# Row totals of the attention weights: every second group of four steps summed into one tile by GpSimd

## The chip, the cores and the metric

One core of one Trainium2 chip runs the whole program. The metric is the device time of one execution in microseconds (us); the kernel before is shown by three timed runs and by one profiled execution. The engines are TensorE (PE, its weight loads PEld), VectorE (DVE), ScalarE (ACT), GpSimd (POOL) and SyncE (SP), which only issues transfers here.

## The reference, cut to what matters

The program is one transformer block: a modulated layer norm, causal attention with 32 heads of 32 channels over 2048 rows, a ten-row adapter prefix, a projection, and then a mixture of 8 experts of which each row takes two. Only the attention matters here:

```
scores = einsum('bhqd,bhkd->bhqk', q, k) / sqrt(hd)
scores = where(causal, scores, -inf)
attn   = softmax(scores, axis=-1)
y      = einsum('bhqk,bhkd->bhqd', attn, v)
```

The softmax is computed as exp(score - row maximum), and y is divided at the end by the total of these weights over all keys of a row. The change is in how that total is formed.

## The kernel before

The attention function works on 4 heads at a time (HG = 4) and on two such head groups in one pass of its outer loop, which runs 4 times. A pass has 8 units (`UNITS`): two head groups times four chunks of 512 query rows. A unit with chunk number qc has 4 * (qc + 1) steps, one for each block of 128 keys, so a pass has 80 steps (`STEPS`): 4, 8, 12 and 16, twice. In each unit the last four steps lie on the diagonal: they work on 512, 384, 256 and 128 query columns (`first_column`). There are 320 steps in all.

A step does this, in the order of its queues:
- PE computes the scores of 4 heads (`score`, L1089, and on the diagonal a small mask matmul, L1093) into three PSUM banks. After each it does one matmul of the look-ahead (`look`, `see`, L1066): it computes the scores of a later unit again, only for their row maximum, into three other PSUM banks (`seen`). DVE takes the maximum of each (`largest`, L1233 and L1239) and frees the bank.
- ACT writes exp of the scores into `prob`, a ring of four steps (`RING = 4`, L1201). Step s overwrites what step s - 4 left, so ACT must wait until PE and POOL have read that.
- PE multiplies the weights of the step two before with v (`multiply`, L1107), four heads at once in four strips of 32 columns of the array.
- For the totals, POOL adds the `prob` of an even step and of the odd step after it into a tile `two` (`add_two`, L1331), in two instructions of two heads each (1024 elements a partition, or 512 on the narrow end of the diagonal). Ahead of a pair on the diagonal it clears the columns that the second step lacks (L1328). PE then adds `two` up over the keys by a matmul with a matrix of ones into `total` (`add_up`, L1120), four steps after the pair's last one, in odd steps only. `two` has two buffers: POOL may start pair p only when PE has read pair p - 2.

Once in a unit: ACT copies y and the total out of PSUM; transfers turn the total into a tile in which DVE inverts it and spread it again; DVE multiplies y by the inverse and adds the adapter's part (`divide`, L1277 and L1280, eight steps after the unit's end); POOL splits the result into two parts (`split`, L1337 and L1339) and SP stores them.

Every queue is written out by hand and runs in order. POOL's order in a step is: `finish` (the second half of the last pair in even steps, then a split if one is due), and then the first half of the new pair in odd steps.

## Time and profile before

| what | value |
|---|---|
| median of 3 timed runs | 2748.73 us (2748.05 to 2749.51) |
| profiled execution, its own time | 2739.68 us |
| its span | 2737.9 us |
| PE busy over the span | 91% |
| DVE, ACT, POOL busy over the span | 59%, 39%, 48% |
| mean granted PE clock | 0.949 |

The span runs from the first to the last instruction of the profiled execution, the own time is the device time of the same execution. Attention's steps run from about 882 us to 1980 us of the span. Busy shares are means over stages that have different limits.

### The profile page before, as it was taken

How to read it: one execution, taken by the hardware profiler on the slowest of the kernel's cores; microseconds unless marked ns; L12 is line 12 of the kernel's file. 1: busy time of each engine (PE TensorE's matmuls, PEld its weight loads, DVE VectorE, ACT ScalarE, POOL GpSimd, SP SyncE). 2: the span in 40 equal slices, each digit the busy share in tenths (PEclk: the TensorE clock that was granted, in tenths of full speed). 3: DMA queues.
4: the chain of work that ended last, by engine and by line, in shares of the span. 5: the costliest groups of instructions: out<-in, count | busy, mean ns of one | idle time of the engine just before them, and what ended most of it. 6: DMA issues, size and time to landing. Idle time of an engine off the chain costs nothing. (4 is left out here: it accounts for less than half of the span.)

```text
span 2737.9 us, 40036 instructions
## 1 busy us (share of the span) xinstructions
PE 2484.4 (91%) x13407; PEld 1621.3 (59%) x13407; DVE 1628.2 (59%) x3253; ACT 1055.2 (39%) x1885; POOL 1321.3 (48%) x827
## 2 busy tenths in 40 slices
PE   6789999998758999999999999999879976999996
PEld 4667677777534444444444444444358765888885
DVE  5544555110458777777777777778226654676666
ACT  3421011111331555555555555556501112444443
POOL 4352342000432767676767676667724452333333
PEclk9899999999885999999999999999989977999998
DMA  7356655312743515151515151522176745878875
GB/s 264 108 160 194 180 167 168 93 39 58 259 134 82 132 40 129 44 131 42 130 42 129 43 128 45 120 48 78 48 227 215 184 101 199 306 276 284 295 283 199
DMA packets 231902, 397.20 MB, mean 145 GB/s; under 512 B 44540, under 2 KB 95292, under 8 KB 231620
## 3 DMA queue, kind: packets, MB, share of 16 engines
q1 hardware_dynamic: 204340, 319.62, 40.1%
q0 software_dynamic: 17152, 50.38, 5.3%
q10 hardware_dynamic: 10256, 25.21, 2.8%
q8 instruction: 88, 1.44, 0.2%
q14 instruction: 66, 0.54, 0.1%
HBM read 299.22 MB, written 103.76 MB: 147 GB/s over the span
## 5 line engine op out<-in xcount | busy, mean ns | idle before, releaser
L1201 ACT ACTIVATE t_prob<-t_scores_psum 128x512 f32<-128x512 f32 (+3 forms) x1280 | 610.0, 538 | 435.7 <-PE t_scores_psum L1093 241.9
L1331 POOL TENSOR_TENSOR t_two<-t_prob 128x1024 f32<-128x1024 f32 (+1 forms) x321 | 691.1, 2175 | 165.6 <-ACT t_prob L1201 111.6
L1233 DVE TENSOR_REDUCE t_part<-t_seen_psum 128x1 f32<-128x512 f32 x768 | 479.0, 681 | 141.3 <-PE t_seen_psum L1066 137.2
L1066 PE MATMUL t_seen_psum<-t_k_stack,t_q_stack 97*128 97x512 f32 (+3 forms) x1283 | 522.0, 419 | 40.3 <-DVE t_q_stack L1221 22.5
L1089 PE MATMUL t_scores_psum<-t_q_stack,t_k_stack 98*128 98x512 f32 (+3 forms) x1280 | 502.8, 404 | 9.1 <-ACT t_prob L1201 7.8
L1089 PEld LDWEIGHTS t_scores_psum<-t_q_stack,t_k_stack 98*128 98x128 f32 x1280 | 241.9, 190 | 306.8 <-ACT t_prob L1201 168.7
L1066 PEld LDWEIGHTS t_seen_psum<-t_k_stack,t_q_stack 97*128 97x128 f32 x1283 | 256.7, 201 | 91.8 <-DVE t_part L1233 37.8
L1239 DVE CUSTOM_DVE_ANT_0 t_seen_psum<-t_seen_psum,t_causal 128x128 f32<-128x128 f32 (+3 forms) x515 | 250.4, 504 | 100.7 <-PE t_seen_psum L1066 89.5
L1107 PE MATMUL t_y_acc_psum<-t_prob,t_v 128*32 128x512 f32 (+3 forms) x2576 | 301.5, 540 | 0.0
L1602 PE MATMUL z_acc_psum<-z_e_hi,z_x_hi 128*128 128x512 f32 x576 | 228.1, 396 | 0.0
L1604 PE MATMUL z_acc_psum<-z_e_hi,z_x_lo 128*128 128x512 f32 x576 | 224.9, 390 | 0.0
L1603 PE MATMUL z_acc_psum<-z_e_lo,z_x_hi 128*128 128x512 f32 x576 | 224.6, 390 | 0.0
L602 PE MATMUL f_acc_psum<-hT_hi,f_w_hi 128*128 128x512 f32 x512 | 207.2, 405 | 2.6 <-POOL f_w_lo L472 2.2
L603 PE MATMUL f_acc_psum<-hT_lo,f_w_hi 128*128 128x512 f32 x512 | 202.0, 395 | 0.0
L604 PE MATMUL f_acc_psum<-hT_hi,f_w_lo 128*128 128x512 f32 x512 | 201.7, 394 | 0.0
L482 POOL TENSOR_TENSOR f_y<-f_y,f_y_hi 128x512 fp32r<-128x512 f32 x64 | 83.8, 1310 | 217.4 <-ACT f_y_hi L264 217.1
L264 ACT ACTIVATE f_y_hi<-f_y 128x512 fp32r<-128x512 f32 x64 | 40.4, 631 | 330.5 <-DVEq L411 330.4
L1120 PE MATMUL t_total_psum<-t_two,t_ones 128*32 128x512 f32 (+1 forms) x1296 | 154.9, 550 | 1.9 <-POOL t_two L1331 1.9
L1828 DVE SCALAR_TENSOR_TENSOR z_x_in<-z_acc_psum,z_ids_a,z_gb 128x1024 f32<-128x1024 f32 x36 | 46.0, 1279 | 140.5 <-DMA z_ids_a<-scratch_table 140.5
L1672 ACT ACTIVATE z_x_hi<-z_turned_psum 128x1024 fp32r<-128x1024 f32 x38 | 38.7, 1018 | 224.5 <-PE z_turned_psum L1588 224.5
L1551 PE MATMUL z_acc_psum<-p_hi,z_y_hi 128*128 128x512 f32 x256 | 102.3, 400 | 23.6 <-DMA z_y_lo<-scratch_y_lo 23.6
L1604 PEld LDWEIGHTS z_acc_psum<-z_e_hi,z_x_lo 128*128 128x128 f32 x576 | 108.4, 188 | 23.0
(234 smaller groups left out, 3894.7 us busy)
## 6 DMA issues: line engine op xcount, KB each, us to landing
z_raw<-in_expert_w SPq DMA_DIRECT2D x80, 512.0 KB, 6.7
z_spare<-in_expert_w SPq DMA_DIRECT2D x72, 512.0 KB, 7.3
f_w_raw<-in_wmod SPq DMA_DIRECT2D x8, 2048.0 KB, 9.9
t_q_stack<-scratch_q_hi SPq DMA_DIRECT2D x64, 256.0 KB, 5.0
t_k_stack<-scratch_k_hi SPq DMA_DIRECT2D x64, 256.0 KB, 5.3
f_w_raw<-in_w_attn SPq DMA_DIRECT2D x24, 512.0 KB, 6.9
t_inverse<-scratch_inverse SPq DMA_DIRECT2D x132, 64.0 KB, 2.0
t_y<-scratch_a_y SPq DMA_DIRECT2D x33, 256.0 KB, 4.6
```

The lines of the kernel that those rows point to most:

```text
L602: nc.tensor.matmul(acc[:, n % 2], lhs[0], rhs[0], start=(k == 0), stop=False)
L603: nc.tensor.matmul(acc[:, n % 2], lhs[0], rhs[1], start=False, stop=False)
L1066: nc.tensor.matmul(seen[:, n % BANKS, 0:width], q_stack[par][0:SEEN, h, t0:t0 + P], k_stack[par][0:SEEN, h, c * CH:c * CH + width], start= ...
L1089: last = nc.tensor.matmul(scores[:, score_bank(step, h), c0:CH], k_stack[par][0:TOPS, h, kt * P:(kt + 1) * P], q_stack[par][0:TOPS, h, qc ...
L1107: last = nc.tensor.matmul(y_acc[h * D:(h + 1) * D, c0:CH], v[par][:, kt, h * D:(h + 1) * D], prob[:, step % RING, h, c0:CH], start=(kt == ...
L1201: nc.scalar.activation(prob[:, step % RING, h, c0:CH], scores[:, score_bank(step, h), c0:CH], ACT.Exp, scale=1.0 / math.sqrt(D)).then_inc( ...
L1233: nc.vector.tensor_reduce(dst, seen[:, n % BANKS], AX.X, ALU.max).then_inc(seen_free, 1)
L1239: nc.vector.tensor_tensor_reduce(out=at, in0=at, in1=causal[:, CH - width:CH], scale=1.0, scalar=MASKED, op0=ALU.add, op1=ALU.max, accum_o ...
L1331: nc.gpsimd.tensor_tensor(two[:, pair % 2, heads, c0:CH], a, b, ALU.add).then_inc(two_ready, 1)
L1602: nc.tensor.matmul(acc[:, s, col], x_hi[:, s, k], e_hi[:, k, col], start=(k == 0), stop=False)
L1603: nc.tensor.matmul(acc[:, s, col], x_hi[:, s, k], e_lo[:, k, col], start=False, stop=False)
L1604: last = nc.tensor.matmul(acc[:, s, col], x_lo[:, s, k], e_hi[:, k, col], start=False, stop=(k == KC - 1))
```

## The change

The 80 steps of a pass are now taken in 20 groups of four (`QUADS`). An odd-numbered group is done as before: two sums of two steps each. An even-numbered group (`long`) becomes one sum of four steps: POOL adds the first two steps as before, then adds the third and the fourth step into the same tile (`add_more`, two instructions for each step, each over the columns that the step has), and PE adds the tile up once, four steps after the group's last step. A pass so has 30 sums where it had 40, and 100 POOL additions where it had 80. In each pass the even groups are 0, 2, 10 and 12, which are a unit's diagonal, and 4, 6, 8, 14, 16 and 18, which have 512 columns in all steps. ACT's waits follow: step s waits for what has been added of step s - 4.

```diff
-                if step % 2 == 1:
-                    add_up(i, (step - TOTAL_LAG - 1) // 2)
+                quad, at = divmod(step - TOTAL_LAG, 4)
+                if at == 3:
+                    add_up(i, quad, 0 if long(quad) else 1)
+                elif at == 1 and not long(quad):
+                    add_up(i, quad, 0)
...
-                    if step % 2 == 0:
-                        act.wait_ge(two_ready, (i * PAIRS + step // 2) * 2 + 2)
+                    quad, at = divmod(step - RING, 4)
+                    if at != 1 and (at != 3 or long(quad)):
+                        act.wait_ge(two_ready, i * HALVES + halves_of(quad) + {0: 2, 2: 4, 3: 6}[at] + 4)
...
+            def add_more(i, quad, x, half):
+
+                n = i * SUMS + sum_of(quad)
+                c0 = first_column(4 * quad + x)
+                heads = slice(half * HALF, (half + 1) * HALF)
+                pool.wait_ge(exp_done, (i * STEPS + 4 * quad + x) * HG + (half + 1) * HALF + BANKS)
+                pool.wait_ge(two_ready, i * HALVES + halves_of(quad) + 2 * (x - 2) + half + 1 + 4)
+                at = two[:, n % 2, heads, c0:CH]
+                nc.gpsimd.tensor_tensor(at, at, prob[:, (4 * quad + x) % RING, heads, c0:CH], ALU.add).then_inc(two_ready, 1)
...
             def finish(i, step):
-                if step % 2 == 0:
-                    add_two(i, step // 2 - 1, 1)
+                quad, at = divmod(step - 2, 4)
+                if at == 0:
+                    add_two(i, quad, 0, 1)
+                elif at == 1 and long(quad):
+                    add_more(i, quad, 2, 0)
+                    add_more(i, quad, 2, 1)
+                elif at == 2 and i * STEPS + step > 0:
+                    if long(quad):
+                        add_more(i, quad, 3, 0)
+                        add_more(i, quad, 3, 1)
+                    else:
+                        add_two(i, quad, 1, 1)
                 for wi in ended(i, step, SPLIT_LAG):
                     split(i, wi)
...
-                    if step % 2 == 1:
-                        add_two(i, step // 2, 0)
+                    if step % 4 == 1:
+                        add_two(i, step // 4, 0, 0)
+                    if step % 4 == 3 and not long(step // 4):
+                        add_two(i, step // 4, 1, 0)
```

POOL's queue, from the pairs of steps 12 to 17 of the first pass (the row with x6) to the pair of steps 22 and 23; group 4 is steps 16 to 19, and steps 20 to 23 are the diagonal of the same unit. Before:

```order
L1331 TENSOR_TENSOR t_two<-t_prob 128x1024 x6
L1337 CAST t_y_own<-t_y 128x512
L1339 TENSOR_TENSOR t_y<-t_y,t_y_own 128x512
L1331 TENSOR_TENSOR t_two<-t_prob 128x1024 x2
L1328 MEMSET t_prob 128x4x128
L1331 TENSOR_TENSOR t_two<-t_prob 128x1024 x2
L1328 MEMSET t_prob 128x4x128
L1331 TENSOR_TENSOR t_two<-t_prob 128x2x256 x2
```

The same piece of POOL's queue in the changed kernel, where L1344 is `add_two`, L1354 `add_more`, L1340 the clearing and L1362 and L1364 the split:

```order
L1344 TENSOR_TENSOR t_two<-t_prob 128x1024 x6
L1354 TENSOR_TENSOR t_two<-t_two,t_prob 128x1024 x2
L1362 CAST t_y_own<-t_y 128x512
L1364 TENSOR_TENSOR t_y<-t_y,t_y_own 128x512
L1354 TENSOR_TENSOR t_two<-t_two,t_prob 128x1024 x2
L1340 MEMSET t_prob 128x4x128
L1344 TENSOR_TENSOR t_two<-t_prob 128x1024 x2
L1340 MEMSET t_prob 128x4x128
L1344 TENSOR_TENSOR t_two<-t_prob 128x2x256 x2
```

Two instructions of 1024 elements in `two` (steps 18 and 19 into one buffer) have become four, and the split now stands between the additions of step 18 and those of step 19.

PE's queue at the end of step 21 of the same pass, before:

```order
L1073 MATMUL t_seen_psum<-t_ident,t_top 16x128
L1066 MATMUL t_seen_psum<-t_k_stack,t_q_stack 128x512
L1107 MATMUL t_y_acc_psum<-t_prob,t_v 32x512 x4
L1120 MATMUL t_total_psum<-t_two,t_ones 32x512 x4
L1089 MATMUL t_scores_psum<-t_q_stack,t_k_stack 128x256
```

And in the changed kernel, where the same functions stand five lines further down:

```order
L1078 MATMUL t_seen_psum<-t_ident,t_top 16x128
L1071 MATMUL t_seen_psum<-t_k_stack,t_q_stack 128x512
L1112 MATMUL t_y_acc_psum<-t_prob,t_v 32x512 x4
L1094 MATMUL t_scores_psum<-t_q_stack,t_k_stack 128x256
```

The four matmuls of the sum of steps 16 and 17 are gone from step 21; the one sum of group 4 stands at the end of step 23, where the sum of steps 18 and 19 stood.

## Rows read from the trace of the kernel before

**Rows 1.** The page, part 1: busy us (share), instructions.

```profile
PE 2484.4 (91%) x13407; PEld 1621.3 (59%) x13407; DVE 1628.2 (59%) x3253; ACT 1055.2 (39%) x1885; POOL 1321.3 (48%) x827
```

**Rows 2.** Windows of attention: width, then busy of the engines (instructions), PE clock.

```profile
core 0: us, PE busy (x) PEld busy (x) DVE busy (x) ACT busy (x) POOL busy (x), PEclk, DMA share, GB/s
1000.00:1200.00 200.00, 197.35 (x1286) 95.47 (x1283) 148.90 (x341) 116.17 (x247) 140.89 (x85) 1.00 0.35 84
...
1900.00:1950.00 50.00, 44.20 (x280) 18.10 (x283) 23.58 (x53) 34.30 (x69) 40.58 (x20) 1.00 0.27 76
```

**Rows 3.** Timeline of PE, steps 17 to 19 of the second pass.

```profile
1210.78 1.06 PE L1107 MATMUL t_y_acc_psum<-t_prob,t_v 128*32 128x512 f32 x8
1211.66 1.04 PE L1120 MATMUL t_total_psum<-t_two,t_ones 128*32 128x512 f32 x8
...
1214.55 1.06 PE L1107 MATMUL t_y_acc_psum<-t_prob,t_v 128*32 128x512 f32 x8
...
1217.46 1.06 PE L1107 MATMUL t_y_acc_psum<-t_prob,t_v 128*32 128x512 f32 x8
```

**Rows 4.** Timeline of PE, steps 12 to 15: after a diagonal.

```profile
1194.98 0.64 PE L1107 MATMUL t_y_acc_psum<-t_prob,t_v 128*32 128x256 f32 x8
1197.63 0.43 PE L1107 MATMUL t_y_acc_psum<-t_prob,t_v 128*32 128x128 f32 x8
...
1200.93 1.06 PE L1107 MATMUL t_y_acc_psum<-t_prob,t_v 128*32 128x512 f32 x8
...
1204.89 0.61 PE L1120 MATMUL t_total_psum<-t_two,t_ones 128*32 128x256 f32 x8
```

**Rows 5.** Groups of POOL by form, 880 to 1990 us: busy, mean ns.

```profile
L1331 POOL TENSOR_TENSOR t_two<-t_prob 128x1024 f32<-128x1024 f32 x256 | 608.6, 2399 | 162.9 <-ACT t_prob L1201 111.6 <-PE t_total_psum L1120 48.7
L1331 POOL TENSOR_TENSOR t_two<-t_prob 128x512 f32<-128x512 f32 x64 | 81.3, 1290 | 2.6
```

**Rows 6.** Timeline of POOL, second pass: steps 17 to 22, then 25 and 29.

```profile
1212.88 4.74 POOL L1331 TENSOR_TENSOR t_two<-t_prob 128x1024 f32<-128x1024 f32 x2 [1.40 <-PE t_total_psum L1120]
1219.06 0.61 POOL L1337 CAST t_y_own<-t_y 128x512 fp32r<-128x512 f32 x1 [1.44 <-DVE t_y L1280]
...
1221.00 4.71 POOL L1331 TENSOR_TENSOR t_two<-t_prob 128x1024 f32<-128x1024 f32 x2
1226.96 0.53 POOL L1328 MEMSET t_prob<- 128x512 f32 x1 [1.25 <-PE t_total_psum L1120]
1227.57 4.73 POOL L1331 TENSOR_TENSOR t_two<-t_prob 128x1024 f32<-128x1024 f32 x2
...
1239.55 4.75 POOL L1331 TENSOR_TENSOR t_two<-t_prob 128x1024 f32<-128x1024 f32 x2 [3.41 <-ACT t_prob L1201]
...
1253.09 4.74 POOL L1331 TENSOR_TENSOR t_two<-t_prob 128x1024 f32<-128x1024 f32 x2 [1.40 <-PE t_total_psum L1120]
```

**Rows 7.** Timeline of ACT: the exps of steps 21 and 24.

```profile
1223.20 1.76 ACT L1201 ACTIVATE t_prob<-t_scores_psum 128x384 f32<-128x384 f32 x4 [1.12 <-PE t_scores_psum L1093]
...
1233.38 2.07 ACT L1201 ACTIVATE t_prob<-t_scores_psum 128x512 f32<-128x512 f32 x4 [2.17 <-PE t_scores_psum L1089]
```

**Rows 8.** Timeline of DVE: the divides at steps 19 and 31.

```profile
1217.05 1.12 DVE L1277 TENSOR_TENSOR t_y_own<-t_y_own,t_inverse 128x512 f32<-128x512 f32 x1
1218.20 0.69 DVE L1280 TENSOR_TENSOR t_y<-t_y,t_y_own 128x512 f32<-128x512 f32 x1
...
1257.26 1.12 DVE L1277 TENSOR_TENSOR t_y_own<-t_y_own,t_inverse 128x512 f32<-128x512 f32 x1
```

**Rows 9.** Timeline of POOL and DVE, 1944 to 1951 us.

```profile
1944.88 5.15 POOL L1331 TENSOR_TENSOR t_two<-t_prob 128x1024 f32<-128x1024 f32 x2 [0.96 <-PE t_total_psum L1120]
1945.56 2.25 DVE L1277 TENSOR_TENSOR t_y_own<-t_y_own,t_inverse 128x512 f32<-128x512 f32 x1 [4.76 <-DMA t_inverse<-scratch_inverse]
1948.59 1.99 DVE L1280 TENSOR_TENSOR t_y<-t_y,t_y_own 128x512 f32<-128x512 f32 x1 [0.78 <-DMA t_y<-scratch_a_y]
```

More of the change, by code:

```diff
@@ L828, in attention @@
     ITEMS = sum(items_of(qc) for _, qc in UNITS) + W
-    PAIRS = STEPS // 2
     RING = 4
+    QUADS = STEPS // 4
+    long = lambda quad: quad % 2 == 0
+    SUMS = 3 * QUADS // 2
+    HALVES = 5 * QUADS
+    sum_of = lambda quad, late=0: quad // 2 * 3 + (quad % 2) + late
+    halves_of = lambda quad: quad // 2 * 10 + (quad % 2) * 6
     Y_LAG, TOTAL_LAG, INV_LAG, DIVIDE_LAG, A_LAG, SPLIT_LAG, STORE_LAG = 2, 4, 5, 8, 6, 8, 9
@@ L1110, in multiply, with add_up @@
                 last.then_inc(y_done, 1)
-            def add_up(i, pair):
-                wi, kt = steps[2 * pair]
-                c0 = first_column(2 * pair)
-                pe.wait_ge(two_ready, (i * PAIRS + pair) * 2 + 6)
-                if kt == 0:
+            def add_up(i, quad, late):
+                wi, kt = steps[4 * quad]
+                last_sum = late or long(quad)
+                n = i * SUMS + sum_of(quad, late)
+                c0 = first_column(4 * quad + 2 * late)
+                pe.wait_ge(two_ready, i * HALVES + halves_of(quad) + (6 if long(quad) else 2 * late + 2) + 4)
+                if (kt, late) == (0, 0):
                     pe.wait_ge(total_free, i * W + wi + 1)
                 for h in range(HG):
-                    last = nc.tensor.matmul(total[h * D:(h + 1) * D, c0:CH], ones[:, :], two[:, pair % 2, h, c0:CH],
-                                            start=(kt == 0), stop=(kt == steps_of(UNITS[wi][1]) - 2))
+                    last = nc.tensor.matmul(total[h * D:(h + 1) * D, c0:CH], ones[:, :], two[:, n % 2, h, c0:CH],
+                                            start=(kt == 0 and not late), stop=(kt == steps_of(UNITS[wi][1]) - 4 and bool(last_sum)))
                 last.then_inc(total_done, 1)
@@ L1308, in _ @@
             pool.sem_inc(y_lo_done, 1)
-            pool.sem_inc(two_ready, 3)
+            pool.sem_inc(two_ready, 4)
             for b in range(2):
@@ L1315, in _, with add_two @@
             pool.wait_ge(sums_set, 2)
-            def add_two(i, pair, half):
-                c0 = first_column(2 * pair)
+            def add_two(i, quad, late, half):
+                n = i * SUMS + sum_of(quad, late)
+                first = 4 * quad + 2 * late
+                c0, c1 = first_column(first), first_column(first + 1)
                 heads = slice(half * HALF, (half + 1) * HALF)
                 if half == 0:
-                    pool.wait_ge(exp_done, (i * STEPS + 2 * pair + 1) * HG + HG + BANKS)
-                    pool.wait_ge(total_done, i * PAIRS + pair + 1)
-                    c1 = first_column(2 * pair + 1)
+                    pool.wait_ge(exp_done, (i * STEPS + first + 1) * HG + HG + BANKS)
+                    pool.wait_ge(total_done, n + 1)
                     if c1 > c0:
                         pool.sem_inc(marks, 1)
-                        nc.gpsimd.memset(prob[:, (2 * pair + 1) % RING, :, c0:c1], 0.0).then_inc(cleared, 1)
-                        pool.wait_ge(cleared, (i * W + steps[2 * pair][0]) * (TPC // 2) + (c0 > 0) + 1)
-                a, b = (prob[:, (2 * pair + x) % RING, heads, c0:CH] for x in range(2))
-                nc.gpsimd.tensor_tensor(two[:, pair % 2, heads, c0:CH], a, b, ALU.add).then_inc(two_ready, 1)
+                        nc.gpsimd.memset(prob[:, (first + 1) % RING, :, c0:c1], 0.0).then_inc(cleared, 1)
+                        clear[0] += 1
+                        pool.wait_ge(cleared, clear[0])
+                a, b = (prob[:, (first + x) % RING, heads, c0:CH] for x in range(2))
+                nc.gpsimd.tensor_tensor(two[:, n % 2, heads, c0:CH], a, b, ALU.add).then_inc(two_ready, 1)
+            def add_more(i, quad, x, half):
[6 more added lines that the diff above has]
+                nc.gpsimd.tensor_tensor(at, at, prob[:, (4 * quad + x) % RING, heads, c0:CH], ALU.add).then_inc(two_ready, 1)
+            clear = [0]
             def split(i, wi):
```

4 lines of the change are left out of this document (2 added, 2 removed).

## The prediction

> **What bounds the kernel now.** I read the page first: PE is busy for 91% of the span, the other three compute engines for 39 to 59% [rows 1]. Attention is one stage of several, so I read it apart, by windows: there PE is busy for 197.35 of 200 us at a granted clock of 1.00, DVE for 149 and POOL for 141 [rows 2]. The reader sees a stage set by PE, with POOL at 70% and DVE at 74%. A busy PE row only says that matmuls overlap, so the real price of a sum has to come from the period of the steps, in the timeline of PE. From the v matmul of step 17 to that of step 18, with a sum between them, it is 1214.55 - 1210.78 = 3.77 us; from step 18 to step 19, with no sum, 1217.46 - 1214.55 = 2.91 us [rows 3]. A sum over 512 columns costs PE 0.86 us, and nothing else of the period changes.
>
> The next view is the timeline of POOL. An addition of 1024 elements takes 2.40 us by itself and a pair of them 4.71 to 4.75 [rows 5, 6], so 2.36 each in a row. Two adjacent steps with one sum last 3.77 + 2.91 = 6.68 us, and POOL has 4.74 of work in them. The mean share hides that this slack is used: POOL's rows end in waits for PE's sums, for the split's input and for exps [rows 6], and each of these gaps is where the next transfer of work would have to go.
>
> **What is removed on PE.** A pass has 20 groups of four steps, and ten of them lose a sum. Six of these have 512 columns (groups 4, 6, 8, 14, 16, 18): 6 x 4 passes = 24 times 0.86 = 20.6 us. Four are a unit's diagonal (0, 2, 10, 12). There the 512 column sum disappears from the odd step after the unit, and the 256 column sum two steps later grows to 512 columns, which is 1.04 - 0.61 = 0.43 us more [rows 3, 4]. The period with the sum that disappears is 1200.93 - 1197.63 = 3.30 us, the one before it, with no sum, is 1197.63 - 1194.98 = 2.65 us [rows 4]; that step has the same look-ahead matmuls and the narrow v matmul, so DVE and ACT hold it there. At most 0.65 is gained and 0.43 is given back: 0.2 each, 16 times, 3.2 us. If the removed sum counted in full, 0.43 each, it would be 6.9.
>
> **What is added on POOL.** A full long group has two more additions of 1024 elements, 4.72 us; 24 of them make 113 us. A diagonal one trades two of 512 (1.29 each [rows 5]) for two of 512 and two of 256, and loses a clearing of 0.53: about 1 us each, 16 in all. POOL's busy time in attention rises by some 130 us over about 1,100, from 70% to some 82%. As a mean that still fits. What decides is whether it fits at each place where ACT waits for it: step s overwrites `prob` of step s - 4.
>
> **The place where it doesn't fit.** Take group 4 (steps 16 to 19) and group 5 (20 to 23). Before: the pair of 16 and 17 starts on POOL at 1212.88, then it idles for the split's input, splits from 1219.06 to 1221.00 (1.94 us), adds 18 and 19, idles, clears from 1226.96 (0.61 to the next start) and adds 20 and 21 until 1227.57 + 4.73 = 1232.30 [rows 6]. The exp of step 24 overwrites step 20. It starts at 1233.38 and its row names PE as what it waited for [rows 7], so there is a slack of 1.08 us. After: POOL has 16 and 17 (4.74), 18 (4.72), the split (1.94), 19 (4.72), the clearing (0.61) and 20 and 21 (4.73), one behind the other. The start stays at 1212.88, since it hangs on the sum of 12 and 13, which stays where it is. The inputs are all there in time: step 18's exps have ended when 16 and 17 are added, and step 21's by 1223.20 + 1.76 = 1224.96 [rows 7]. The chain ends at 1212.88 + 21.46 = 1234.34. That is 0.96 us after the exp of step 24 started before, though PE would by then be 0.86 us earlier. So in this group the whole gain is lost and 1.0 us more.
>
> **The port that POOL and DVE share.** The timeline of POOL and DVE late in attention shows a price that the means don't. DVE's multiply of the divide takes 2.25 us beside an addition of POOL, and the add behind it 1.99 us [rows 9], where it takes 0.69 when POOL idles [rows 8]. The ends tell the rule: POOL's first addition ends at 1944.88 + 2.40 = 1947.28 and the multiply at 1947.81; POOL's second ends at 1950.03 and the add at 1950.58. Each time DVE has waited for the end of POOL's instruction and then needed 0.55 us. POOL's pair took 5.15 instead of 4.74, 0.41 more, for the multiply in its middle. At step 19 the multiply of 1217.05 took 1.12: it waited for POOL's pair to end (1217.62); the add found POOL idle, because POOL's next instruction was the split, which waits for that very add [rows 6, 8]. After the change POOL adds step 18 there. The multiply ends as before at 1218.17, but POOL's addition starts 0.41 late; the add is ready at 1218.20 and must wait for the end of that addition, so it ends some 2 us later than before and again costs POOL 0.41. The Trainium skill, SBUF — State Buffer, section Terms, calls this pair of ports "Lock-allocated, exclusive, held for the full instruction". The trace agrees; by the rule alone each divide would find POOL's port held more often in the changed kernel, which speaks against moving adds to POOL, and the sum would come out on the slow side as mine does.
>
> With 2 x 0.41 the chain at group 4 ends at 1235.2, 1.8 us after 1233.38. DVE's 2 us reach PE too through the three look-ahead banks, but they run beside the same chain and don't add to it. PE is tied to that exp: its fourth score waits for the first exp of the step. Groups 14 and 15 have the same shape (a split at step 59). Two places in each of 4 passes: 8 x 1.8 = 14.6 us, in which the 0.86 is already counted.
>
> **The places with a late divide only.** The units that end at steps 23 and 63 are split at steps 31 and 71, in the group behind the long groups 6 and 16. Before, the divide at 1257.26 waits for the end of the pair started at 1253.09 and then has the port, ending at about 1259.1 [rows 6, 8]. After, POOL adds 24 and 25, 26, and 27 without a pause from 1239.55 and starts 28 and 29 at 1253.7, which end at 1258.5. The multiply is asked for 0.86 us earlier, waits for 1258.5, and the add behind it ends at about 1259.7, 0.6 us later than before, while PE was to be 0.86 earlier: DVE is 1.5 us later against PE. The three banks absorb at most a part. I take the gain as lost and 0.5 us more, 8 times: +4. Bounds: -0.86 each if the banks absorb all (-6.9), +1.3 each if they absorb nothing and the delay is added on the earlier steps (+10).
>
> **The rest.** The 8 remaining full long groups (8 and 18) have no split near and keep 0.86: -6.9. The last 40 steps have little look-ahead; POOL is busy there for 40.58 of 50 us already [rows 2], and the end of attention hangs on the same queue. I take +3, between 0 and the 8 us that its extra 15 us of additions less its idle time would give.
>
> **Sum.** 14.6 + 4 - 6.9 - 3.2 + 3 = 11.5 us. The profiled execution took 2739.68 us and would take 2751.2. The median of the timed runs is 9 us above it, so I scale: 2748.73 + 11.5 = 2760.3.
>
> **What has no row.** An addition in place (`two` is input and output) is not in the trace. It has two inputs and one output of the same size as the others; the nearest rows are the pair additions (2.36) and the split's subtraction, 512 elements, also in place. Below it can't be, as nothing is saved; above I allow 0.2 us. The added waits of POOL are on its own older instructions and cost nothing when met.
>
> **The rivals.**
> - *The late divide doesn't reach PE* (0.12). The look-ahead banks absorb it at steps 31 and 71: -6.9 in place of +4, and +1 for +3: 11.5 - 10.9 - 2 = -1.4 us, 2747. For it: DVE is idle a quarter of the time. Against: PE waits when the fourth bank is wanted, within a step.
> - *Faster* (0.19). POOL and DVE don't collide as I read it, because the divide falls into another phase. The 8 bad places then cost 1.0 each: 7.7 - 6.9 - 6.9 - 3.2 + 1 = -8.3 us, 2740 (0.12). If POOL's chain also fits, 20.6 + 3.2 = 24 us are gained, 2725 (0.07). It decides at group 4: the chain of 21.46 us would have to be 1.8 us shorter (0.96 + 0.86), that is each of its eight additions 2.1 us instead of 2.36. No row shows one of this size so short.
> - *POOL becomes the bound* (0.17). If an addition in place takes 0.2 us more, each long group is 0.8 longer; at 8 places this adds 6.4 us, and the slack of groups with a diagonal behind them (8 and 18, some 0.5 us after their clearing) goes too: 16 or more groups at 0.8, 2775 to 2785.
> - The forecast itself: 0.52.
>
> **How the numbers follow.** A measurement of this kernel tells about 0.2%, 5.5 us, from no change. Of the forecast (2755 to 2767) nearly all lies above 2754.2: slower 0.49 and same 0.03. The first rival is same, 0.12; of the rival at 2740 about 0.05 is same and 0.07 faster, the one at 2725 faster; the last is slower, 0.17. Together: faster 0.14, same 0.20, slower 0.66. The range leaves out the fastest cases and the top of the last rival: 2743 to 2776.
>
> **What the next profile would show.** PE: in full long groups no outside split the step without a sum has a period of 2.91 instead of 3.77; 120 sums instead of 160. ACT: at steps 24 and 64 of a pass its exps wait for POOL's `two`, 2 to 4 us. DVE: the divide's two instructions take 1.5 to 2.7 us in most units, and PE has look-ahead matmuls that wait for DVE at steps 19, 31, 59 and 71. POOL: some 82% busy, additions in a row of 2.36 us. The prediction is wrong if ACT doesn't wait for POOL, if the in-place additions take another time, or if the divide stays at 1.8 us.

## The result, and the profile of the changed kernel

The changed kernel took 2785.56 us (median of 4 runs, 2773.79 to 2793.74), the kernel before 2749.12 us beside it (2748.05 to 2752.34). The ratio is 1.0116, with an interval of 1.009 to 1.0143: 36 us slower, where the forecast said 11.5 us and the range ended at 2776. In a later comparison the same changed kernel took 2772.29 us (2768.17 to 2783.96) against 2745.65, a ratio of 1.008 [1.0048, 1.0112], 27 us slower. So the sign was right and the size was not: two or three times the forecast.

The page of the changed kernel, part 1 and the slices of part 2 for PE, POOL and the granted clock:

```profile
PE 2506.4 (90%) x13087; PEld 1631.4 (58%) x13087; DVE 1674.2 (60%) x3253; ACT 1060.0 (38%) x1885; POOL 1449.6 (52%) x890
...
PE   6789999998759999999999999999859985999997
...
POOL 4452342001342887878788878787923543233323
PEclk9999999999977999999999999999979986999998
```

Against [rows 1] PE has 320 instructions fewer (the 40 sums of 8 matmuls) and yet 22 us more of busy time; DVE has 46 us more with the same count; POOL has 128 us more, as forecast (130). Fewer matmuls with more busy time are slower matmuls. The next view is attention by windows: the columns are the width, then busy us of PE, PEld, DVE, ACT and POOL, the granted clock of PE, and what DMA did. First the kernel before, over the same stretch:

```profile
882.00:1960.00 1078.00, 1054.58 (x6733) 503.04 (x6737) 781.11 (x1845) 635.99 (x1323) 767.59 (x439) 1.00 0.35 85
```

The changed kernel:

```profile
882.00:1960.00 1078.00, 1031.26 (x6220) 494.20 (x6219) 804.84 (x1835) 612.24 (x1268) 854.64 (x480) 0.97 0.34 81
```

PE's clock is at 0.97 on average and no longer at 1.00, and PE idles for 47 us in place of 23. Counted from the first to the last v matmul, attention takes 1139.3 us where it took 1095.0: 44.3 us more. (First and last mean the starts at 879.29 and 1974.28 us before, and at 882.33 and 2021.64 us after.) The profiled execution of the changed kernel was also the slowest of its four, 2793.74 us, 8 us above their median, and that of the kernel before, 2739.68 us, lies 9 us below its median. So the two profiles are 54 us apart where the medians are 36, and the 44.3 us are probably nearer to the top of what the change costs than to its middle. What follows after attention took 770.3 us in the one and 763.6 us in the other, and that part has the same code.

**The place that the prediction was about.** The timeline of POOL at group 4, third pass (the rows of the kernel before are of the second):

```profile
1511.90 4.73 POOL L1344 TENSOR_TENSOR t_two<-t_prob 128x1024 f32<-128x1024 f32 x2 [1.41 <-PE t_total_psum L1127]
1516.59 5.60 POOL L1354 TENSOR_TENSOR t_two<-t_two,t_prob 128x1024 f32<-128x1024 f32 x2
1522.14 0.60 POOL L1362 CAST t_y_own<-t_y 128x512 fp32r<-128x512 f32 x1
1522.82 1.28 POOL L1364 TENSOR_TENSOR t_y<-t_y,t_y_own 128x512 fp32r<-128x512 f32 x1
1524.06 4.72 POOL L1354 TENSOR_TENSOR t_two<-t_two,t_prob 128x1024 f32<-128x1024 f32 x2
1528.72 0.53 POOL L1340 MEMSET t_prob<- 128x512 f32 x1
1529.32 4.72 POOL L1344 TENSOR_TENSOR t_two<-t_prob 128x1024 f32<-128x1024 f32 x2
```

ACT and DVE there:

```profile
1534.12 2.06 ACT L1212 ACTIVATE t_prob<-t_scores_psum 128x512 f32<-128x512 f32 x4 [3.20 <-POOL t_two L1344]
...
1516.10 1.08 DVE L1288 TENSOR_TENSOR t_y_own<-t_y_own,t_inverse 128x512 f32<-128x512 f32 x1
1518.63 1.33 DVE L1291 TENSOR_TENSOR t_y<-t_y,t_y_own 128x512 f32<-128x512 f32 x1 [1.45 <-DMA t_y<-scratch_a_y]
```

POOL has no gap from 1511.90 to 1534.04, and the exp of step 24 now names POOL as what it waited for. From the start of the pair to that exp it is 1534.12 - 1511.90 = 22.22 us; before it was 1233.38 - 1212.88 = 20.50 [rows 6, 7]. That is 1.72 more, against the forecast of 1.8. Both additions of step 18 are stretched by the divide, 5.60 for the two where two undisturbed ones take 4.72. The 1.45 us ahead of DVE's addition are a wait for the transfer of the adapter's part.

PE shows how that reaches it. Steps 19 and 20 begin with their v matmuls, and between them a look-ahead matmul waits for DVE:

```profile
1516.51 1.07 PE L1112 MATMUL t_y_acc_psum<-t_prob,t_v 128*32 128x512 f32 x8
...
1520.55 0.39 PE L1071 MATMUL t_seen_psum<-t_k_stack,t_q_stack 97*128 97x256 f32 x1 [1.14 <-DVE t_part L1250]
...
1522.17 1.07 PE L1112 MATMUL t_y_acc_psum<-t_prob,t_v 128*32 128x512 f32 x8
```

This step lasts 5.66 us, 1.5 more than before, where it is 4.14 from 1217.46 [rows 3] to the next v matmul:

```profile
1221.60 1.06 PE L1107 MATMUL t_y_acc_psum<-t_prob,t_v 128*32 128x512 f32 x8
```

The sum of step 21 is gone (-0.86), and step 23 waits for POOL (+1.0): 1.7 in all. In the fourth pass it is 1.4. In the first two the clock had fallen behind step 19 (more on this below), and step 23 is then as long as before.

At steps 59 to 63, which have the same shape, another wait comes in. In the first three passes they take 2.1, 2.9 and 3.3 us more than before, at full clock, and at step 63 PE stands 1.35, 2.12 and 2.60 us, not for POOL but for the transfer that brings the row maxima of the next unit into `q_stack`. From the list of waits of the changed kernel, over attention:

```profile
PE t_scores_psum L1094 <- DMA t_q_stack<-t_minus_top: 6.1, 3, 2.6
```

The kernel before has no such wait. In the first pass SP issued this transfer 1.1 us later against the v matmul of step 63 than before, and by the records of its semaphore it landed 5.9, 6.7 and 7.2 us after the last issue, where it took 2.8 to 3.4 before. No run takes it apart from the rest, so why it lands late stays open.

**The place that it was not about.** The timeline of PE at step 51, third pass; here a unit's divide falls to DVE in group 12, which is a long group with a diagonal. Rows of the v matmuls of steps 49 to 54 and of the wait among them, and behind them DVE's addition of the divide:

```profile
1624.29 1.06 PE L1112 MATMUL t_y_acc_psum<-t_prob,t_v 128*32 128x512 f32 x8
1627.19 0.85 PE L1112 MATMUL t_y_acc_psum<-t_prob,t_v 128*32 128x384 f32 x8
...
1631.85 0.51 PE L1071 MATMUL t_seen_psum<-t_k_stack,t_q_stack 97*128 97x512 f32 x1 [2.06 <-DVE t_part L1244]
1633.54 1.08 PE L1112 MATMUL t_y_acc_psum<-t_prob,t_v 128*32 128x256 f32 x8
1638.26 0.66 PE L1112 MATMUL t_y_acc_psum<-t_prob,t_v 128*32 128x128 f32 x8
1642.56 1.55 PE L1112 MATMUL t_y_acc_psum<-t_prob,t_v 128*32 128x512 f32 x8
1646.12 1.07 PE L1112 MATMUL t_y_acc_psum<-t_prob,t_v 128*32 128x512 f32 x8
```

```profile
1629.53 1.66 DVE L1291 TENSOR_TENSOR t_y<-t_y,t_y_own 128x512 f32<-128x512 f32 x1 [1.25 <-DMA t_y<-scratch_a_y]
```

DVE first stands 1.25 us for the transfer of the adapter's part and then needs 1.66 us for an addition that takes 0.69 when POOL idles [rows 8]; the look-ahead matmul waits behind both.

The same stretch by windows:

```profile
1625.00:1632.00 7.00, 4.94 (x36) 2.40 (x33) 5.18 (x7) 2.20 (x6) 6.26 (x5) 1.00 0.72 163
1634.00:1644.00 10.00, 10.00 (x40) 5.37 (x32) 6.33 (x10) 5.13 (x9) 4.55 (x4) 0.52 0.53 133
1644.00:1650.00 6.00, 5.94 (x35) 3.10 (x32) 3.74 (x6) 3.47 (x7) 1.58 (x2) 1.00 0.00 0
```

PE has stood for 2 us, and then, with no gap in its own work, it is granted half its speed (0.52 over these 10 us: 1.2 GHz in place of 2.4) and is back at 1.00 after them. Steps 52 and 53 last 4.72 and 4.30 us; steps 12 and 13, of the same shape at full clock, last 2.65 and 3.30 in [rows 4], the second with a sum that is gone here. Over steps 52 to 54 the loss is 4.1 us, twice the stop that came first. A reader who looks at busy time alone sees a saturated PE in those 10 us, and the list of waits has only the 2.06 us ahead of them.

The clock records have one such stretch inside attention in the kernel before, 6.8 us long, and nine in the changed one, 85 us in all.

### The profile page after: what moved, and what is told of

Same layout as the page of the kernel before. It is cut to its first block and busy times, and to the rows that moved or that the text cites. A ratio compares the mean times of both kernels' runs of the same rounds, so it can differ in the third digit from the quotient of the medians.

```text
span 2791.9 us, 39580 instructions
## 1 busy us (share of the span) xinstructions
PE 2506.4 (90%) x13087; PEld 1631.4 (58%) x13087; DVE 1674.2 (60%) x3253; ACT 1060.0 (38%) x1885; POOL 1449.6 (52%) x890
## 5 line engine op out<-in xcount | busy, mean ns | idle before, releaser
L1344 POOL TENSOR_TENSOR t_two<-t_prob 128x1024 f32<-128x1024 f32 (+1 forms) x240 | 532.6, 2241 | 144.8 <-ACT t_prob L1212 122.8
L1071 PE MATMUL t_seen_psum<-t_k_stack,t_q_stack 97*128 97x512 f32 (+3 forms) x1283 | 536.0, 430 | 61.3 <-DVE t_q_stack L1232 22.5
L1094 PE MATMUL t_scores_psum<-t_q_stack,t_k_stack 98*128 98x512 f32 (+3 forms) x1280 | 516.1, 414 | 17.9 <-ACT t_prob L1212 9.7
L1094 PEld LDWEIGHTS t_scores_psum<-t_q_stack,t_k_stack 98*128 98x128 f32 x1280 | 249.0, 195 | 326.9 <-ACT t_prob L1212 188.1
L1071 PEld LDWEIGHTS t_seen_psum<-t_k_stack,t_q_stack 97*128 97x128 f32 x1283 | 264.0, 206 | 118.5 <-DVE t_part L1244 43.6
L1112 PE MATMUL t_y_acc_psum<-t_prob,t_v 128*32 128x512 f32 (+3 forms) x2576 | 312.7, 559 | 0.0
L1354 POOL TENSOR_TENSOR t_two<-t_two,t_prob 128x1024 f32<-128x1024 f32 (+2 forms) x160 | 302.0, 1916 | 0.0
L1127 PE MATMUL t_total_psum<-t_two,t_ones 128*32 128x512 f32 (+1 forms) x976 | 120.7, 566 | 4.3 <-POOL t_two L1344 4.3
```

Of the source, the lines that this page charges most:

```text
L1071: nc.tensor.matmul(seen[:, n % BANKS, 0:width], q_stack[par][0:SEEN, h, t0:t0 + P], k_stack[par][0:SEEN, h, c * CH:c * CH + width], start= ...
L1094: last = nc.tensor.matmul(scores[:, score_bank(step, h), c0:CH], k_stack[par][0:TOPS, h, kt * P:(kt + 1) * P], q_stack[par][0:TOPS, h, qc ...
L1112: last = nc.tensor.matmul(y_acc[h * D:(h + 1) * D, c0:CH], v[par][:, kt, h * D:(h + 1) * D], prob[:, step % RING, h, c0:CH], start=(kt == ...
L1344: nc.gpsimd.tensor_tensor(two[:, n % 2, heads, c0:CH], a, b, ALU.add).then_inc(two_ready, 1)
L1354: nc.gpsimd.tensor_tensor(at, at, prob[:, (4 * quad + x) % RING, heads, c0:CH], ALU.add).then_inc(two_ready, 1)
```

## The experiments

Each comparison ran beside the kernel before, whose medians were 2746.43, 2745.81 and 2745.65 us for the three sets. Beside the ratio I give attention by itself, from the profiled execution: it is the stage that the change touches, and what lies behind it varies with the values where a kernel leaves work out, since the routing of tokens then comes out otherwise. "Low" is the number and the length of the stretches at 1.2 GHz within it. The last column takes out what these stretches cost, at 0.39 us for each us beyond the 6.8 of the kernel before; where the 0.39 comes from stands below the first pair of experiments.

| kernel | median us | ratio (95%) | attention | less before | low | left |
|---|---|---|---|---|---|---|
| before | 2745.65 to 2749.12 | | 1095.0 | | 1, 6.8 us | 0 |
| changed | 2785.56 | 1.0116 [1.009, 1.0143] | 1139.3 | +44.3 | 9, 85.3 | +13.7 |
| changed_again | 2772.29 | 1.008 [1.0048, 1.0112] | 1136.6 | +41.6 | 11, 88.7 | +9.6 |
| long_8_18 | 2738.10 | 0.9976 [0.9955, 0.9997] | 1088.2 | -6.8 | 2, 6.8 | -6.8 |
| long_5_8_15_18 | 2741.35 | 0.9979 [0.9962, 0.9997] | 1096.8 | +1.8 | 4, 23.9 | -4.8 |
| long_4_14 | 2771.02 | 1.0081 [1.005, 1.0112] | 1128.5 | +33.5 | 10, 58.0 | +13.5 |
| long_6_16 | 2748.32 | 1.0005 [0.9985, 1.0026] | 1105.9 | +10.9 | 5, 27.3 | +2.9 |
| long_diagonals | 2751.71 | 1.0027 [1.0006, 1.0047] | 1104.5 | +9.5 | 2, 23.9 | +2.9 |
| dve_late_2 | 2743.88 | 1.0002 [0.9977, 1.0027] | 1100.3 | +5.3 | 2, 13.7 | +2.6 |
| dve_late_4 | 2754.63 | 1.0036 [1.0013, 1.0059] | 1110.8 | +15.8 | 4, 27.3 | +7.8 |
| before_one_input | 2754.85 | 1.0037 [1.002, 1.0054] | 1102.2 | +7.2 | 4, 23.9 | +0.5 |
| one_input_divide | 2769.18 | 1.0096 [1.0061, 1.0132] | 1105.0 | +10.0 | 7, 44.4 | -4.6 |
| small_split | 2806.44 | 1.0205 [1.0159, 1.0252] | 1122.6 | +27.6 | 9, 68.3 | +3.6 |
| one_input_small_split | 2778.30 | 1.0121 [1.0082, 1.016] | 1080.5 | -14.5 | 2, 13.7 | -17.2 |

### Which long groups cost, and which pay

Theory A is the one of the prediction, completed by the clock: a long group whose additions share POOL's queue with a split and DVE's divide loses, and one that doesn't gains 0.86 us. The rival B says that every long group loses alike, through POOL's busy time. The kernel long_8_18 makes only groups 8 and 18 long, long_4_14 only groups 4 and 14.

```diff
-    long = lambda quad: quad % 2 == 0
+    LONG = [8, 18]
+    long = lambda quad: quad % QUADS in LONG
-    SUMS = 3 * QUADS // 2
-    HALVES = 5 * QUADS
...
+    SUMS = 2 * QUADS - len(LONG)
+    HALVES = 4 * QUADS + 2 * len(LONG)
...
```

> Only groups 8 and 18 of a pass are sums of four steps (8 groups in 4 passes, 16 more additions on GpSimd). These have no split and no divide beside them. Theory A (the loss comes from places: a split inside the long group, a divide that waits for the port, and TensorE's clock that falls after such a stop): no such place is made, so 8 x 0.86 = 6.9 us are gained, 2742 us, and the granted clock in attention stays as before. Rival B (the loss is spread: every addition more on GpSimd costs the kernel time): a fifth of the 40 long groups, so about a fifth of the loss, +7 us, 2756 us.

Measured: 2738.10 us, ratio 0.9976, and attention 6.8 us shorter. Steps 37 and 77 of each pass lost 0.84 to 0.86 us each, and no other step changed in the same way in all passes. A holds. With its interval just below 1 this kernel beats the one before as well as the changed one; long_5_8_15_18, further down, has the same two groups and gives the same ratio.

> Only groups 4 and 14 of a pass are sums of four steps, again 8 groups in 4 passes and the same 16 more additions; here a split and a divide fall into the long group and a diagonal follows. Theory A: 8 x 1.8 = 14 us, and on top what a fallen clock costs where the stop is long enough, 0 to 5 us at each of 8 places: 2763 to 2790 us. Rival B: as with groups 8 and 18, +7 us, 2756 us.

Measured: 2771.02 us, ratio 1.0081; attention 33.5 us longer. B falls: eight long groups here cost 33.5 us and eight there give 6.8. But 8 places x 1.7 us are only 13.6. The other 19.9 us go with the clock: ten stretches, 58.0 us, against 6.8. That is 19.9 / 51.2 = 0.39 us for each us at 1.2 GHz. For the changed kernel the direct costs, added up step by step further down, are 13.9 us, and (44.3 - 13.9) / (85.3 - 6.8) = 0.39 too. Both go by 1.7 us for every place, also for those where the low clock hid a part of it. Single stretches, read by themselves, give a little more: 4.1 us of 10.2 at step 51 above, which is 0.40, and 3.0 us of 6.8 in dve_late_4 below, 0.44. At 0.44 the clock would have 34.5 of the 44.3 us and the direct costs 9.8. The five runs of long_4_14 have a mean granted clock of 0.940 to 0.942, the 24 of the kernel before beside them 0.943 to 0.953.

### Can a stop of PE alone bring the low clock?

Only with this shown is the clock a cause and not an accompaniment. The kernels dve_late_2 and dve_late_4 are the kernel before with two or four idle reductions on DVE ahead of one divide of each pass (the one at step 51). No sum moves and POOL gets no work. Theory A: PE stops at step 51, and the clock falls behind it. Rival C: it falls through something of POOL's or of the sums, and here nothing but the stop is seen.

```diff
             def divide(i, wi):
                 ...
+                for _ in range(4 if wi == 4 else 0):
+                    nc.vector.tensor_reduce(waste[:, :], inverse[:, :], AX.X, ALU.max).then_inc(waste_done, 1)
+                    waste_n[0] += 1
+                    dve.wait_ge(waste_done, waste_n[0])
                 ...
```

> The same with four extra reductions, about 2.8 us. Theory A: the stop reaches TensorE in all 4 passes, 4 x (2 + 4): +15 to +28 us, with a low-clock stretch at step 51 of each pass in the trace. Rival C: 4 x 2 = +8 us and no more low-clock stretches than before.

Measured: 2754.63 us, ratio 1.0036; attention 15.8 us longer. The timeline of PE in dve_late_4 at step 51 of the first pass, the v matmuls and the wait ahead of them:

```profile
1058.88 0.50 PE L1068 MATMUL t_seen_psum<-t_k_stack,t_q_stack 97*128 97x512 f32 x1 [2.38 <-DVE t_part L1235]
1061.04 1.08 PE L1109 MATMUL t_y_acc_psum<-t_prob,t_v 128*32 128x256 f32 x8
1065.76 0.66 PE L1109 MATMUL t_y_acc_psum<-t_prob,t_v 128*32 128x128 f32 x8
1069.32 1.06 PE L1109 MATMUL t_y_acc_psum<-t_prob,t_v 128*32 128x512 f32 x8
```

and its windows:

```profile
1062.00:1069.00 7.00, 7.00 (x36) 4.51 (x32) 3.75 (x6) 4.02 (x8) 3.07 (x3) 0.69 0.71 162
1069.00:1075.00 6.00, 6.00 (x38) 2.69 (x36) 4.39 (x8) 3.54 (x8) 3.39 (x2) 1.00 0.00 0
```

The same picture as in the changed kernel: a stop, then a full PE at a lower clock, and step 52 lasts 1065.76 - 1061.04 = 4.72 us. It is there in each of the four passes: step 51 is longer by 2.2, 1.8, 1.2 and 2.2 us, steps 52 and 53 together by another 2.4, 3.0, 3.0 and 3.1. Rival C falls: a late DVE is enough. The size was below what I had written, 16 us in attention and 9 in the median, since each stretch was 6.8 us long here, where it is up to 13.7 in the changed kernel.

> The kernel before, unchanged but for two extra reductions on VectorE (512 elements, about 0.7 us each) ahead of the divide of the unit that ends at step 43, so that VectorE is about 1.4 us later at step 51, once in each of 4 passes. Nothing else is touched: GpSimd has its old additions. Theory A (a stop of TensorE in attention is followed by a stretch at 1.2 GHz): if the look-ahead banks absorb the 1.4 us, nothing; if the stop reaches TensorE, 1 us directly and about 4 us for a low-clock stretch of 7 to 10 us, in each pass: 0 to +20 us, and steps 52 and 53 of a pass 2.1 and 1.0 us longer where it falls. Rival C (the low-clock stretches have to do with GpSimd's load): no low-clock stretch appears, at most +4 us.

Measured: 2743.88 us, ratio 1.0002, no difference; attention 5.3 us longer. Step 51 was delayed by 0.2 to 1.3 us, and the clock fell behind it in two of the four passes. In one of these the longest wait of a look-ahead matmul in that step was 1.18 us; in the third pass there was one of 1.74, and the clock stayed. So the length of one stop doesn't decide it alone, and what does stays open.

### The port, the split, and both

The changed kernel was then run with what I held to be the causes taken out. In one_input_divide the two operations of the divide have one input (so the result lacks the division and the addition); in small_split the two operations of the split on POOL treat 8 columns instead of 512. The control before_one_input is the kernel before with the same divide.

```diff
-                nc.vector.tensor_tensor(own, own, inverse[:, :], ALU.mult).then_inc(norm_step, 1)
+                nc.vector.tensor_reduce(own, own.rearrange("p (n a) -> p n a", a=1), AX.X, ALU.max).then_inc(norm_step, 1)
...
-                nc.gpsimd.tensor_tensor(y_lo.bitcast(F32R), y[:, :], y_hi, ALU.subtract).then_inc(y_lo_done, 1)
+                nc.gpsimd.tensor_tensor(y_lo[:, 0:8].bitcast(F32R), y[:, 0:8], y_hi[:, 0:8], ALU.subtract).then_inc(y_lo_done, 1)
...
```

> The kernel before with the same two one-operand instructions in the divide (the division and the adapter's part left out): the control. There the multiply waits some 0.4 us for the port in most of the 32 units and the look-ahead hides it. Both theories: 0 to -3 us, 2746 to 2749 us.

> The changed kernel, but the two instructions of the divide on VectorE read one SBUF operand each (a copy written as a reduction over one element); left out are the division by the total and the adapter's part. Theory A: VectorE no longer waits for GpSimd's port; the waits of the look-ahead matmuls at steps 19, 31, 51, 59 and 71 go and with them most low-clock stretches in attention; what stays is exp waiting for GpSimd at steps 24 and 64, about 1 us each. 2740 to 2755 us; the attention stage 35 to 45 us shorter than in the changed kernel. Rival B: nothing changes, 2780 to 2790 us.

Measured: both totals missed, 2754.85 and 2769.18 us. The control has nothing of the sums changed and lies 0.37% above the kernel before; its profiled execution is 2756.17 - 2739.68 = 16.5 us longer than that of before, of which attention has 7.2 (6.7 of them from the clock's stretches), what lies ahead of it 2.1 and what lies behind it 7.1. Behind it other values are routed: a line of the expert matmuls has 608 of them where before it has 576. (With the values unchanged, that part took 756.9 to 770.3 us in these profiles.) As to attention, the stage in question, one_input_divide took 1105.0 us, 34 less than the changed kernel, where I had written 35 to 45, and 3 more than the control. Steps 11, 19 and 51 got back to their former length or below it in 7 of 12 cases. In the others DVE's addition stood for the transfer of the adapter's part, which it reaches sooner now; the lists of waits have, for the changed kernel and then for one_input_divide:

```profile
DVE t_y L1291 <- DMA t_y<-scratch_a_y: 11.5, 13, 1.6
...
DVE t_y L1291 <- DMA t_y<-scratch_a_y: 24.0, 19, 2.4
```

Step 23 still waited for POOL and was 0.9 to 1.7 us longer than before. Step 63 was 2.1 to 3.3 us longer in three passes and 0.8 shorter in the fourth, and in the three PE stood for the transfer of the row maxima, 5.9 us in all. So that wait doesn't need the port.

The groups of POOL in that stage, by form, for the changed kernel (busy us, mean ns):

```profile
L1344 POOL TENSOR_TENSOR t_two<-t_prob 128x1024 f32<-128x1024 f32 x208 | 492.2, 2388 | 143.5 <-ACT t_prob L1212 122.8 <-PE t_total_psum L1127 18.1
L1354 POOL TENSOR_TENSOR t_two<-t_two,t_prob 128x1024 f32<-128x1024 f32 x96 | 233.7, 2461 | 0.0
```

and for one_input_divide:

```profile
L1344 POOL TENSOR_TENSOR t_two<-t_prob 128x1024 f32<-128x1024 f32 x208 | 492.2, 2388 | 133.2 <-ACT t_prob L1212 106.0 <-PE t_total_psum L1127 24.7
L1354 POOL TENSOR_TENSOR t_two<-t_two,t_prob 128x1024 f32<-128x1024 f32 x96 | 227.9, 2403 | 0.0
```

An addition in place takes 2403 ns where no divide collides with it, as long as one from two other buffers. The 58 ns more in the changed kernel are the port: 96 x 0.058 = 5.6 us, where 8 places with two collisions of 0.41 each would be 6.6.

> The changed kernel with the two instructions of the split on GpSimd cut to 8 of 512 columns (the rest of the high and low part of y is left as it was), so that some 1.7 us of the 1.94 go out of GpSimd's queue. Theory A: the chain at groups 4 and 14 ends 1.7 us sooner, exp at steps 24 and 64 waits little or not; but VectorE's divide still waits for the port. The 1.0 to 1.4 us at steps 23 and 63 go (8 times, 9 us) with the low-clock stretches that began there: 2765 to 2780 us. Rival D (the split has no part in it; the additions alone fill the chain): nothing changes, 2785 us.

> The changed kernel with both: one-operand instructions in the divide and the split cut to 8 columns (left out: the division, the adapter's part and most of the split). All 40 long groups and all 80 additions more are still there. Theory A: neither the port nor the chain holds anything, so the sums' whole gain shows against the kernel before with one-operand instructions: 24 x 0.86 = 20.6 us in attention less a little at steps 23 and 63, attention 1075 to 1085 us, the kernel 2730 to 2742 us. Rival B (the additions themselves cost time): attention stays above 1100 us.

Measured: small_split 2806.44 us, one_input_small_split 2778.30 us, both totals outside what I had written. As in the control, other values reach the routing, and what lies behind attention took 800 and 813 us in place of the 764 of before. Attention itself: 1122.6 us with the small split alone, where step 23 is as long as before and the stop at step 19 stayed (1.1 to 1.6 us), with the low clock behind it in three passes (in such passes step 23 isn't longer in the changed kernel either, so only the fourth pass shows what the split does there); and 1080.5 us with both, within the 1075 to 1085 expected. That kernel makes all the additions of the changed one, 852 us of POOL in 1078:

```profile
882.00:1960.00 1078.00, 1049.38 (x6501) 498.02 (x6497) 772.66 (x1844) 644.19 (x1345) 852.06 (x508) 0.99 0.35 85
```

It is 14.5 us shorter than before, 21.7 shorter than its control. So POOL's busy share, the same as in the changed kernel (854.64), isn't what costs. By the last column the one-input divide takes 13.7 - (-4.6) = 18.3 us off, the small split 10.1, and both 30.9, a little over their sum. The gain of the 40 removed sums is real, and the two kinds of place where POOL meets others eat it.

### The other groups, and the changed kernel once more

> Only groups 6 and 16 are sums of four steps: the divide falls beside additions in the short group behind. In the changed kernel these places gave 0.86 us back at step 29 and cost 1.04 at step 31. Theory A: +0.2 us each, 8 times, +1.5 us, and no low-clock stretch, as the stop is short: 2746 to 2752 us. Rival B (each addition costs time): +7 us.

Measured: 2748.32 us, ratio 1.0005. Steps 29 and 69 lose 0.86, steps 31 and 71 get 0.8 to 1.0 longer in seven of eight cases: at most +0.2 a group where I had +0.5 in the prediction. Attention is 10.9 us longer all the same, since the profile has four stretches of low clock more than that of the kernel before. None of them is behind step 31 or 71, so they aren't this change's doing as far as the steps show; that much one execution differs from another.

> Only the diagonal groups 0, 2, 10 and 12 are sums of four steps. In the changed kernel they cost 0.0 us net in the steps of the sums, but step 11 lasted 0.2 to 0.9 us and step 51 1.0 to 1.7 us longer, and the clock fell behind step 51 in three passes of four (3.6 us). Theory A: 4 x (0.5 + 1.3 + 3.6 x 3/4) = +18 us, 2764 us, with low-clock stretches behind step 51. Rival B: 16 groups with few more elements to add, +3 us.

Measured: 2751.71 us, ratio 1.0027. The step where the sum disappears loses 0.49, the one with the grown sum gains 0.43, so a diagonal group is worth 0.06 us and not 0.2. The +18 expected were +6 in the median, nearer to the rival's +3, and +9.5 in attention: step 11 was 0.2 to 0.9 us longer in three passes and 2.5 in the second, and the clock fell behind it only there. Step 51, for which I had expected 1.3 us, was only 0.1, 0.2, -0.3 and 0.6 us longer than before. What it goes with is when the adapter's transfer lands. In the four kernels in which group 12 is long and the divide has two inputs (the changed one twice, small_split, long_diagonals), step 51 of the first three passes lasted 5.06 to 5.09 us where DVE's addition had stood up to 1.02 us for that transfer, and 6.35 to 6.59 us where it had stood 1.18 us or more, in 12 cases of 12. In the kernel before, with nothing of POOL's beside it, a stand of 1.33 us gives 5.41 us.

> Groups 5, 8, 15 and 18: to the two full groups without a split, two diagonal ones that have no divide beside them (5 and 15). Theory A: 8 x 0.86 from the full ones and 8 x 0.0 to 0.4 from the diagonal ones, 7 to 10 us faster than before: 2736 to 2739 us, the same as with 8 and 18 alone or a little less. Rival B: 16 more long groups than none, slower than before by some 5 us.

Measured: 2741.35 us, ratio 0.9979, the same as long_8_18 within the intervals. Groups 5 and 15 are two more diagonals and add 0.06 each, nothing that counts.

> The changed kernel once more, on the same chip as the others of this call, for a second profiled execution. Theory A (low-clock stretches fall by chance behind the same stops): 2773 to 2794 us again, other places and another number of stretches, and the attention stage shorter or longer by about 3.5 us for each stretch less or more. Rival: the same stretches at the same steps.

Measured: 2772.29 us. Eleven stretches at 1.2 GHz, 88.7 us, at partly other steps than in the first profile: behind step 11 in the first two passes here, behind step 51 in all four there. The steps with a sum that is gone or grown are the same to some 0.1 us, and which of the stops brings the low clock differs from execution to execution. The mean granted clock of each run, over the whole program, goes with its time:

```
changed, both sets        2768.17 at 0.942 ... 2773.79 at 0.942 ... 2783.96 at 0.937 ... 2793.74 at 0.937
before, beside the second 2738.34 at 0.951 ... 2745.57 at 0.949 ... 2760.59 at 0.942
long_8_18                 2728.96 at 0.952 ... 2738.10 (median)  ... 2747.98 at 0.944
```

All ten runs of the changed kernel lie at 0.935 to 0.942, those of the kernel before at 0.942 to 0.953, and the fastest of each kernel are at the upper end of its clocks.

The four profiles with group 12 long and a two-input divide also tell how the fall goes with the length of the stop. With the waits of PE for DVE of 0.82 to 0.85 us at steps 11 and 51 of the first three passes, the clock fell in none of 16 cases. With those of 1.14 to 1.17 us at steps 19 and 59 of the same passes (long_diagonals has none) it fell in 11 of 18, and with those of 2.06 us at steps 11 and 51, in all passes, in 10 of 11. In these counts the price of a stop rises faster than its length.

## Why the prediction was wrong in size and right in direction

Point by point, by the steps of the prediction; "measured" is from the periods of the same step in the two profiles, where the clock was full in both.

- **Groups 4, 5, 14, 15: right at the first, not whole at the second.** Forecast 1.8 us a place, measured 1.7 at group 4 (step 19 +1.5, step 21 -0.86, step 23 +1.0). The chain on POOL, the wait of ACT for it and 22.22 us were as worked out, at step 24 of two passes; where the low clock came first, the wait is gone. At steps 59 to 63 it was 2.1 to 3.3 us in three passes, through the transfer of the row maxima, a path that the prediction does not have.
- **The late divide at steps 31 and 71: right in sign, small.** Forecast +0.5, measured at most +0.2.
- **Groups 8 and 18: right.** -0.86 each, and long_8_18 has it alone.
- **The diagonals: forecast -0.2, measured -0.06.** The bound of 0.65 was taken for the gain; the step got 0.49 shorter.
- **"The rest": wrong.** It looked for late divides behind full long groups only. Those of the diagonal groups 2 and 12, at steps 11 and 51, met POOL's additions as well: some 0.6 us and 1.0 us on PE, eight times, about 6.7. How much of this is the change's own stays open: it hangs on when the adapter's transfer lands, and long_diagonals has next to nothing of it at step 51.
- **The port: right** in its rule and its price of 0.41 us. That the divide takes 1.5 to 2.7 us "in most units" was only partly so: its addition took 0.8 to 2.75 us in the units at 11, 19, 51 and 59, and still 0.69 at the others. POOL is busy for 79% of attention (854.64 of 1078 us), forecast 82.

The direct terms are thus 13.6 + 1.5 - 6.9 - 1.0 + 6.7 = 13.9 us (8 places at 1.7 for the first), against the 11.5 forecast. That they come so near is in part luck: the late divides came out 2.5 below their term, and the diagonals and "the rest" 2.2 and 3.7 above theirs. **The step that failed is the sum itself, which took PE's granted clock of 1.00 [rows 2] as given.** It counted a stop as what it lasts. PE's stops also took the clock away behind them, and of the 44.3 us of attention some 10 to 14 are stops and work and 30 to 35 are what matmuls at 1.2 GHz cost. The list of waits showed the stops: in the kernel before, over attention,

```profile
PE t_seen_psum L1066 <- DVE t_part L1233: 11.8, 30, 1.5
...
ACT t_prob L1201 <- POOL t_two L1331: 2.7, 1, 2.7
...
PE t_seen_psum L1066 <- DVE t_part L1239: 0.6, 1, 0.6
```

and in the changed kernel, the same two lines of DVE:

```profile
PE t_seen_psum L1071 <- DVE t_part L1244: 17.9, 31, 2.1
PE t_seen_psum L1071 <- DVE t_part L1250: 15.3, 16, 1.6
```

The kernel before held stops of up to 1.5 us and one stretch of low clock in 1095 us; nothing in it warned of the price, but a term for it was missing and its upper bound was not in the range.

Of the rivals: that the late divide doesn't reach PE was wrong, it reached it in more places than said. That the chain fits was wrong at the places named, and true where the port and the split are taken out (one_input_small_split). The rival "POOL becomes the bound" came close to the measured number, 2775 to 2785, by a cause that isn't there: an addition in place is not slower, and POOL's busy time as such cost nothing.

By the Trainium skill, SBUF — State Buffer, section Terms, DVE and POOL hold their pair of ports for a full instruction. The runs agree: 34 us of attention go when the divide has one input. At 0.39 us for each us at 1.2 GHz, 16 of them are PE's clock and 18 the delay itself; dve_late_4 shows that a delay of DVE alone brings both.

What stays open: which stops bring the low clock, and for how long. The stops of 1.2 to 2.4 us in these runs did so in some passes and not in others. The two medians of the changed kernel, 36 and 27 us above the kernel before, differ in the same direction as its clocks (0.935 to 0.942, then 0.937 to 0.942), but so small a difference of clocks isn't proof. Why the transfer of the row maxima lands late at step 63, and what it adds beyond the 3 us or so of this profile, stays open too. The 0.39 us comes from two kernels and is only assumed for the others; of changed_again it leaves 9.6 us where the same kernel had 13.7, so the last column is good to some 4 us.

## What to carry to other kernels

Work moved to POOL costs where its queue already has something that others wait for, and where DVE's two-input operations meet it, not by its mean share: the same 130 us of additions cost 14 us at one set of places and gave 17 with those two taken out. Beside these two kinds of place there is the transfer behind step 63, which only the traces show. So move it group by group, measure the two or three kinds of place apart, and keep those that pay (here groups 8 and 18: 0.24% faster where the whole change is 1.2% slower). On a PE that is nearly full, price a stop at more than its length, and read the granted clock in the windows behind each stop, since the busy share hides it.

## What the runs showed of the hardware beyond that

Late in attention the changed kernel has a two-input operation of DVE that doesn't get its port at the end of POOL's current instruction but has to wait through several. Timeline of the changed kernel, DVE and POOL:

```profile
1991.39 6.97 DVE L1288 TENSOR_TENSOR t_y_own<-t_y_own,t_inverse 128x512 f32<-128x512 f32 x1 [4.76 <-DMA t_inverse<-scratch_inverse]
...
1993.13 4.67 POOL L1344 TENSOR_TENSOR t_two<-t_prob 128x1024 f32<-128x1024 f32 x2
...
1998.39 0.69 DVE L1291 TENSOR_TENSOR t_y<-t_y,t_y_own 128x512 f32<-128x512 f32 x1
```

It ends at 1998.36, 0.56 us after POOL's pair (1997.80), so it waited through both of its additions and didn't get in between them. A subtraction of 1024 elements (L1313) took 1.22 us at 1999.00 and 11.93 us at 2009.84. In all other places that I read, as at 1516.10, DVE had the port at the next boundary. What decides between the two isn't settled.
